# Expert stage of a decoder layer: first products two ahead of second ones, double buffers, early split of two experts' weights

## The reference, cut to what matters

```python
# x: (1024 tokens, 256), after a layer norm
logits = x @ gate_weight.T ; scores = sigmoid(logits)       # 16 routed experts
# two of four groups of experts by the sum of their two best, then the 4 best experts
weight = scores of the chosen ones / their sum * 2.5        # 0 for the others
y  = (silu(x @ sh_gate_w.T) * (x @ sh_up_w.T)) @ sh_down_w.T    # shared, width 256
for e in range(16):                                             # routed, width 128
    y += weight[:, e] * ((silu(x @ gate_w[e].T) * (x @ up_w[e].T)) @ down_w[e].T)
out = x_residual + y
```

## Time and profile before

| | us |
|---|---|
| median of three runs | 595.95 |
| the profiled execution, its own time | 597.41 |
| its span, first to last instruction | 595.5 |
| TensorE busy | 557.4 |
| ScalarE busy | 398.3 |
| VectorE busy | 437.1 |
| GpSimd busy | 298.9 |

### The profile page before, as it was taken

The page is one execution under the profiler, slowest core; times in us unless marked ns, Lnnn a source line. Parts: engine busy times, 40 slices in busy tenths (PEclk is TensorE's granted clock), DMA queues, the critical chain, the costliest instruction groups (busy, mean ns, idle before and its releaser), DMA issues.

```text
span 595.5 us, 10331 instructions
## 1 busy us (share of the span) xinstructions
PE 557.4 (94%) x3392; PEld 488.2 (82%) x3392; DVE 437.1 (73%) x1046; ACT 398.3 (67%) x783; POOL 298.9 (50%) x201
## 2 busy tenths in 40 slices
PE   3899999999999999999999999897777799999996
PEld 1687889989989989989989988786566688888885
DVE  8778989989989988998998998968593433333334
ACT  4978988878978979879779778665531433343331
POOL 2434756746746646656666563301041655556542
PEclk9998999999999999999999999999998899999999
DMA  6122032032032032032031020110002433333311
GB/s 206 29 107 81 0 117 81 1 116 81 2 117 81 2 116 81 2 116 75 8 116 56 27 97 23 59 29 1 0 1 70 149 105 107 104 123 113 108 62 70
DMA packets 16267, 42.23 MB, mean 71 GB/s; under 512 B 4544, under 2 KB 4800, under 8 KB 16224
## 3 DMA queue, kind: packets, MB, share of 16 engines
q1 hardware_dynamic: 16224, 41.69, 20.9%
HBM read 40.47 MB, written 1.21 MB: 70 GB/s over the span
## 4 chain that ended last, share of the span: by engine, by line
PE 83%; DVE 8%; ACT 4%; DMA 2%; issue 2%; SPq 1%; ACTq 0%; DVEq 0%
PE bank L1258 20%; PE bank L1260 19%; PE bank L1259 19%; PE bank L1254 15%; PE bank L1396 5%; PE bank L1384 4%; ACT tok L624 2%; DMA xbias<-in_xb 1%; DMA w_raw<-in_w 1%; DVE stats L976 1%; DVE xT_lo L911 1%; DVE gated_lo L1158 1%; ACT values L538 0%; DVE x L1248 0%; DVE raw L995 0%
## 5 line engine op out<-in xcount | busy, mean ns | idle before, releaser
L1258 PE MATMUL bank<-xT_lo,w_hi 128*128 128x512 f32 x336 | 140.0, 417 | 3.6 <-DVE conv L1149 1.3
L1260 PE MATMUL bank<-xT_hi,w_hi 128*128 128x512 f32 x336 | 132.3, 394 | 0.0
L1259 PE MATMUL bank<-xT_hi,w_lo 128*128 128x512 f32 x336 | 131.8, 392 | 0.0
L425 POOL TENSOR_TENSOR gated_lo<-gated,gated_hi 128x512 fp32r<-128x512 f32 x30 | 38.7, 1290 | 116.5 <-ACT gated_hi L644 112.8
L624 ACT ACTIVATE tok<-bank,nmr,rstd 128x128 f32<-128x128 f32 x256 | 91.0, 504 | 2.1 <-DVE nmr L891 2.1
L502 POOL TENSOR_TENSOR gate<-conv,tap 128x512 f32<-128x512 f32 x36 | 46.4, 1291 | 84.5 <-DVE conv L1149 71.4
L1258 PEld LDWEIGHTS bank<-xT_lo,w_hi 128*128 128x128 f32 x336 | 63.5, 189 | 18.8 <-DVE conv L995 3.2
L1260 PEld LDWEIGHTS bank<-xT_hi,w_hi 128*128 128x128 f32 x336 | 63.3, 188 | 14.2
L420 POOL TENSOR_TENSOR conv<-tap,conv 128x506 f32<-128x506 f32 x32 | 61.9, 1934 | 21.8 <-DVE conv L995 21.8
L420 POOL TENSOR_TENSOR raw<-tap,raw 128x506 f32<-128x506 f32 x32 | 61.9, 1934 | 20.3 <-DVE raw L995 16.3
L1259 PEld LDWEIGHTS bank<-xT_hi,w_lo 128*128 128x128 f32 x336 | 63.7, 190 | 9.6
(11 more groups left out here) (167 smaller groups left out, 1358.3 us busy)
## 6 DMA issues: line engine op xcount, KB each, us to landing
w_raw<-in_w SPq DMA_DIRECT2D x34, 384.0 KB, 4.4
obet<-obet_rows SPq DMA_DIRECT2D x16, 768.0 KB, 4.2
tap<-route_rows SPq DMA_DIRECT2D x16, 512.0 KB, 3.6
wv_raw<-in_wv SPq DMA_DIRECT2D x8, 256.0 KB, 4.8
wo_raw<-in_wo SPq DMA_DIRECT2D x8, 256.0 KB, 4.9
x<-in_x SPq DMA_DIRECT2D x2, 512.0 KB, 4.6
out_x<-x SPq DMA_DIRECT2D x4, 256.0 KB, 2.4
raw<-in_ctx SPq DMA_DIRECT2D x1, 512.0 KB, 5.4
```

Of the source, the lines that this page charges most:

```text
L425: nc.gpsimd.tensor_tensor(gated_lo[:, cc], gated[:, c * N:(c + 1) * N], gated_hi[:, cc].bitcast(F32), ALU.subtract).then_inc(gated_lo_read ...
L1258: nc.tensor.matmul(o, l_hi, r_lo, start=start, stop=False, skip_group_check=loose)
L1259: nc.tensor.matmul(o, l_lo, r_hi, start=False, stop=False, skip_group_check=loose)
L1260: return nc.tensor.matmul(o, l_hi, r_hi, start=False, stop=stop, skip_group_check=loose)
```

## The change

- The second products run one expert later: TensorE's order in the loop is `gate_up(n+2)`, `down(n)`.
- `silu_g`, `prod`, `act_hi`, `act_lo` and the product with the factors get two buffers (`two`, `weighted`).
- Experts 1 and 2 are not multiplied by a factor; their `act_hi` and `act_lo` are made from `prod`. The memset of ones goes.
- Experts 3 and 4 are split whole into memory that the attention leaves free (`early`), ahead of the last layer norm: ScalarE's `early_high` between `context_soft(1)` and `context_att(1)`, GpSimd's `early_low` after the first addition of the context. The weights of 5 and 6 are loaded right after, and split after `r_ready`.
- GpSimd does nothing from there to `r_ready`.
- ScalarE takes the sigmoid of half 0, the silu of expert 1's half 0, the sigmoid of half 1, the scores' copy, the silu of half 1. TensorE has the transposes of the scores before the last quarter of `gate_up(1)`, and the whole of `gate_up(3)` before `down(2)`.
- In the loop ScalarE's order is `gate_silu(n)`, `gate_up_high(n+1)`, `act_high(n)`, `down_high(n)`; GpSimd's `weigh(n,0)`, `gate_up_low(n+1)`, `weigh(n,1)`, `down_low(n)`; SyncE's factors of n, wait for `down_low(n)`, weights of n+2.

```diff
-        act_w = gate
-        act_hi, act_lo = gated_hi[:, 0:T], gated_lo[:, 0:T]
+        act_hi, act_lo = gated_hi[:, 0:2 * T], gated_lo[:, 0:2 * T]
+        def two(n, c):
+            return slice(n % 2 * T + c * N, n % 2 * T + (c + 1) * N)
+        def weighted(n, c):
+            if n <= E_SHARED:
+                return prod[:, two(n, c)]
+            o = n % 2 * 3 * T + c * N
+            return gate[:, o:o + N]
+        def early(n):
+            return (wv_hi[:, 64:64 + 3 * D], wv_lo[:, 64:64 + 3 * D]) if n == 3 else (
+                wo_hi[:, 0:3 * D], wo_lo[:, 0:3 * D])
...
             load_expert(4, 1)
+            for n in (5, 6):
+                sp.wait_ge(w_lo_ready, n - 2 + H)
+                load_expert(n, 1 - n % 2)
...
-            def load_route(e, s, before):
-                sp.wait_ge(e_weighted, before)
+            def load_route(e, s):
+                if not (isinstance(e, int) and e < 2):
+                    sp.wait_ge(e_weighted, e * NCH - NCH)
...
-            with sp.Fori(0, E_ROUTED // 2 - 1) as r:
+            with sp.Fori(0, E_ROUTED // 2 - 2) as r:
                 for s in range(2):
-                    expert_split(r * 2 + (3 + s))
-                    load_expert(r * 2 + (5 + s), s)
-                    load_route(r * 2 + (2 + s), s, r * (2 * NCH) + NCH * (3 + s))
+                    load_route(r * 2 + (2 + s), s)
+                    sp.wait_ge(down_lo_ready, r * 2 + (s + 1))
+                    load_expert(r * 2 + (7 + s), s)
+            for s in range(2):
+                load_route(E_ROUTED - 2 + s, s)
...
-            pool.wait_ge(p_added, TT // 2)
-            nc.gpsimd.memset(wbc, 1.0).then_inc(ones_ready, 1)
-            pool.wait_ge(ones_ready, 1)
-            weigh(1, 0, True)
-            gate_up_low(3, 0)
-            weigh(2, 1, False)
-            gate_up_low(4, 1)
-            down_low(3, 0)
-            def step(n, s, left=2):
-                pool.wait_ge(ld_route[s], (n - 1 - s) * 8)
-                weigh(n, s, False)
-                if left > 1:
-                    gate_up_low(n + 2, s)
-                if left > 0:
-                    down_low(n + 1, 1 - s)
+            pool.wait_ge(x_mixed, 1)
+            early_low(3)
+            early_low(4)
+            pool.wait_ge(r_ready, 1)
+            gate_up_low(5, 0)
+            gate_up_low(6, 1)
+            def step(n, m, s, up=True, down=True):
+                pool.wait_ge(ld_route[s], n * 8 - (1 + s) * 8)
+                weigh(n, m, s, 0)
+                if up:
+                    gate_up_low(n + 1, 1 - s)
+                weigh(n, m, s, 1)
+                if down:
+                    down_low(n, s)
+            step(3, 3, 0, False, False)
+            step(4, 4, 1, False, False)
+            step(5, 5, 0, False)
+            step(6, 6, 1)
...
             context_soft(1)
+            early_high(3)
+            early_high(4)
             context_att(1)
...
-            gate_silu(1, True, (0,))
+            router_scores(0)
+            gate_silu(1, 1, (0,))
+            router_scores(1)
             act.wait_ge(r_tok_full, 1)
...
+            def step(n, m, s, up=True):
+                gate_silu(n, m)
+                if up:
+                    gate_up_high(n + 1, 1 - s)
+                act_high(n, m)
+                down_high(n, s)
...
-                    u_times(r * 2 + (3 + s))
-                    act_low(r * 2 + (3 + s))
+                    u_times(r * 2 + (7 + s), 7 + s)
+                    act_low(r * 2 + (7 + s), 7 + s)
...
             pe.wait_ge(r_tr_ready, NCH)
-            gate_up(3, 0, chunks=(1,))
             gate_up(4, 1)
-            down(3, 0, False, False)
-            with pe.Fori(0, E_ROUTED // 2 - 1) as r:
+            gate_up(5, 0)
+            down(3, 3, 0)
+            gate_up(6, 1)
+            down(4, 4, 1)
+            with pe.Fori(0, E_ROUTED // 2 - 2) as r:
                 for s in range(2):
-                    gate_up(r * 2 + (5 + s), s)
-                    down(r * 2 + (4 + s), 1 - s, False, False)
-            down(E_ALL, 1, False, True)
+                    gate_up(r * 2 + (7 + s), s)
+                    down(r * 2 + (5 + s), 5 + s, s)
+            down(E_ALL - 1, E_ALL - 1, 0)
+            down(E_ALL, E_ALL, 1)
```

More of the change, by code:

```diff
@@ L488, in down_low @@
                 w = slice(s * 3 * D + 2 * D, (s + 1) * 3 * D)
-                pool.wait_ge(down_hi_ready, n - E_SHARED)
+                pool.wait_ge(down_hi_ready, n - 4)
                 nc.gpsimd.tensor_tensor(w_lo[:, w], w_raw[:, w], w_hi[:, w].bitcast(F32),
                                         ALU.subtract).then_inc(down_lo_ready, 1)
[L493 to L503, removed]
@@ L525, in _, with early_low, weigh @@
-            with pool.Fori(0, E_ROUTED // 2 - 1) as r:
+            def early_low(n):
+                hi, lo = early(n)
+                s = 1 - n % 2
+                pool.wait_ge(w_hi_ready, n + H)
+                nc.gpsimd.tensor_tensor(lo, w_raw[:, s * 3 * D:(s + 1) * 3 * D], hi.bitcast(F32),
+                                        ALU.subtract).then_inc(w_lo_ready, 1)
+            def weigh(n, m, s, c):
+                pool.wait_ge(u_prod, n * NCH + (c + 1 - NCH))
+                if not (isinstance(n, int) and n < 5):
+                    pool.wait_ge(e_hi, n * NCH + (c + 1 - 3 * NCH))
+                    pool.wait_ge(e_lo, n * NCH + (c + 1 - 3 * NCH))
+                nc.gpsimd.tensor_tensor(weighted(m, c), prod[:, two(m, c)],
+                                        wbc[:, s * T + c * N:s * T + (c + 1) * N],
+                                        ALU.mult).then_inc(e_weighted, 1)
@@ L802, in _, with router_scores @@
                 half_out(2, c, xT_hi)
-            for c in range(NCH):
+            def router_scores(c):
                 act.wait_ge(r_full, c + 1)
@@ L1211, in _ @@
             op(nc.vector.tensor_tensor(k4, k4, gm4, ALU.add))
-            act_low(1)
-            u_times(2, chunks=(0,))
+            u_times(2, 2, (0,))
+            act_low(1, 1)
             for t in range(TT):
@@ L1603, in down @@
-            def down(n, s, first, last):
-                if not (isinstance(n, int) and n <= E_SHARED):
-                    pe.wait_ge(down_lo_ready, n - E_SHARED)
-                o = s * 3 * D + 2 * D
-                for t in range(TT):
-                    if t % G == 0:
-                        pe.wait_ge(e_lo, (n - 1) * NCH + t // G + 1)
-                    tt = slice(t * P, (t + 1) * P)
-                    ins = mm3(y_acc[t // 2][:, (t % 2) * D:(t % 2 + 1) * D], act_hi[:, tt], act_lo[:, tt],
-                              w_hi[:, o:o + D], w_lo[:, o:o + D], first and t % 2 == 0, last, loose=True)
-                    if last and t % 2:
-                        ins.then_inc(y_full, 1)
-                if not last:
-                    ins.then_inc(e_down, 1)
+                hi, lo = w_hi[:, s * 3 * D:(s + 1) * 3 * D], w_lo[:, s * 3 * D:(s + 1) * 3 * D]
@@ new lines, in gate_up @@
+                if isinstance(n, int) and n in (3, 4):
+                    hi, lo = early(n)
+                for c, j in parts:
+                    if not (isinstance(n, int) and n == 1):
+                        pe.wait_ge(g_silu if j == 0 else u_prod, n * NCH + (c + 1 - 2 * NCH))
+                    for kt in range(KT):
+                        o = j * D + kt * P
+                        ins = mm3(e_ring[2 * c + j][:, :], hi[:, o:o + P], lo[:, o:o + P],
+                                  xs_(xT_hi, kt, c * N, (c + 1) * N), xs_(xT_lo, kt, c * N, (c + 1) * N),
+                                  kt == 0, kt == KT - 1)
+                    ins.then_inc(e_full, 1)
@@ new lines, in down @@
+            def down(n, m, s, chunks=range(NCH)):
+                hi, lo = w_hi[:, s * 3 * D:(s + 1) * 3 * D], w_lo[:, s * 3 * D:(s + 1) * 3 * D]
+                if m in (3, 4):
+                    hi, lo = early(m)
+                elif m > 4:
+                    pe.wait_ge(down_lo_ready, n - 4)
+                o = 2 * D
+                for c in chunks:
+                    pe.wait_ge(e_lo, n * NCH + (c + 1 - NCH))
+                    for t in range(G * c, G * (c + 1)):
+                        tt = slice(m % 2 * T + t * P, m % 2 * T + (t + 1) * P)
+                        ins = mm3(y_acc[t // 2][:, (t % 2) * D:(t % 2 + 1) * D], act_hi[:, tt], act_lo[:, tt],
+                                  hi[:, o:o + D], lo[:, o:o + D], m == 1 and t % 2 == 0, m == E_ALL, loose=True)
+                        if m == E_ALL and t % 2:
+                            ins.then_inc(y_full, 1)
+                    if m < E_ALL and c == NCH - 1:
+                        ins.then_inc(e_down, 1)
```

163 lines of the change are left out of this document (89 added, 74 removed).

## The result

The changed kernel takes 629.17 us (median of 4 runs, 626.52 to 631.81) against 595.96: 1.054 times the kernel before, 95% interval 1.048 to 1.060. It is slower, as forecast, but by 33 us and not by 18: above the range of 603 to 623. In a later round (e10_after) it took 627.05 (623.98 to 629.55), 1.052 times the kernel before (1.048 to 1.057). The profiled execution took 630.37 us, its span is 628.4.

What follows compares the result with a forecast made beforehand. TensorE, busy 94%, bounds the old kernel; a GpSimd transfer cycle bounds the changed loop. 467.4 + 11 x 10.95 = 587.9, plus 7.3 and 13.9 to 609.1, plus 0.8 and 3.7: span 613.6, forecast 614.0 us, range 603 to 623.

Steps and rivals of the forecast that it cites:

- What bounds the kernel before, and what could be won: TensorE, busy 94% of the span, at 8.27 us per expert; some 13 to 15 us winnable outside the loop.
- TensorE stays the bound: Rival for the expert loop: period stays 8.27 us, factors being there before GpSimd asks; 581.6 us, chance 0.03.
- Part 1: Early split of experts 3 and 4: ScalarE's 1.7 us hidden in idle time, GpSimd's subtractions priced at 0.
- Part 2: Routing stage: short VectorE operations with GpSimd idle, `r_ready` at 445.6 against 451.2; four table loads make TensorE wait 2 us.
- D5: End of the low part of down of expert 5, forecast at 467.4 (467.3 to 467.5).
- Part 3: Stretch from `gate_up(1)` to `down(4)`: no TensorE stall over 0.3 us besides the 2 us, ending about 472.6.
- Part 4: New queue order in the expert loop: factors held back until GpSimd's previous instruction, period 10.95 us, TensorE idle about 2.7.
- the ring: Loop cycle through SyncE's issues, the factors' transfer, GpSimd and ScalarE, independent of TensorE: 10.89 us, 10.95 with waking.
- issue of the weights to the start of `weigh`: Loop term for the second issue and the factors' landing: 4.6 us taken, between 4.0 and 6.0.
- The end: After D16: `gate_up(18)` starts 7.3 us later, last products 13.9 us plus 0.8 for the clock, then 3.7 to span's end.
- D16: End of the low part of down of expert 16, eleven periods after D5, forecast at 587.9.
- the second issue is held up: Rival: each factor transfer issued slowly or landing after 5.6 us; loop period 11.8 to 12.35, 623 to 629, chance 0.12.

Runs made afterwards that it cites:

- e10_after: The changed kernel itself, unaltered, measured again in a later round on the same chip as e9_unrolled: 627.05 us, 1.052 times the kernel before.
- e5_all: Changed kernel with factors issued one step earlier, down's split ahead of the second multiply and act_high, and both sigmoids together: 582.35 us, ratio 0.976.
- e8_busy: e5_all with seven unneeded 128x512 multiplies put on GpSimd in the routing: 586.16 us against 582.35.
- e9_unrolled: Changed kernel with SyncE's loop written out, order unchanged: 618.30 us, ratio 1.037.
- e2_swap: Changed kernel with the two issues behind the wait swapped, factors of n+1 before weights of n+2: 615.26 us, ratio 1.033.
- e1_ahead: Changed kernel with the factors of expert n+1 issued before the wait for down's low part of n: 588.87 us, ratio 0.988.
- e3_sigmoids: Changed kernel with ScalarE's two sigmoids one after the other and the first silu behind them: 624.89 us, ratio 1.047.
- e6_half: Changed kernel loading only the factors of the first 512 tokens, used by both halves: 612.83 us, ratio 1.025.

## Why the prediction was right or wrong

- *What bounds the kernel before, and what could be won*: right. With everything in order (e5_all) the time is 582.35; the rival "TensorE stays the bound" had 581.6.
- *Part 1*, the early split at no cost: right. ScalarE's idle time ahead of `L722` is 0.35 us after, where it was 1.81, and the layer norm isn't later.
- *Part 2*, the routing on VectorE: right. I had `r_ready` at 445.6; it came at 445.48, and `L1228`, the old `L1179`, takes 0.29 us and not 1.22. e8_busy shows that it is GpSimd's idleness that does it.
- *Part 2*, four table loads: the 2 us of waiting came as 1.92, and no drain follows a load, as in the earlier trace rows. Against the 2.8 us more that I had estimated from the Trainium skill (ScalarE: Activation LUTs, "What ACT_TABLE_LOAD costs") the trace of after decides:

```profile
424.71 1.28 ACT L844 ACT_TABLE_LOAD   x1
426.01 0.59 ACT L844 ACTIVATE gate<-bank 16x512 f32<-16x512 f32 x1
426.61 1.28 ACT L813 ACT_TABLE_LOAD   x1
427.91 0.60 ACT L813 ACTIVATE tok<-bank 128x512 f32<-128x512 f32 x1
428.52 1.28 ACT L844 ACT_TABLE_LOAD   x1
429.82 0.59 ACT L844 ACTIVATE gate<-bank 16x512 f32<-16x512 f32 x1
```

- Here a term was missing: the granted clock falls behind this wait (last section). TensorE's order therefore ran 1.3 us late, and the routing weights were ready at 451.15, not 449.9. The trip of the factors over DRAM took 6.94 us, not 5.95; in the other traces with whole factors it varies from 5.6 to 8.0. Together D5 is 469.55 instead of 467.4: 2.15 us.
- *Part 3*, the stretch to `down(4)`: right. TensorE has no wait there besides the 1.92 us, and ends `down(4)` near 474.1, where I had 472.6; `gate_up(2)` already ended 1.3 us late.
- *Part 4*, the ring: right in what it goes through, and in its independence of TensorE. It was mis-sized. The sum had 10.95; the mean of eleven periods is 11.81:

| term | predicted | measured |
|---|---|---|
| end of down's low part to issue of the weights | 0.18 | 0.17 |
| distance of the two issues | 0.40 | 0.75 (0.62 and 0.90 in turn) |
| issue of the factors to `weigh` | 4.26 | 4.71 |
| GpSimd's and ScalarE's work to the end of down's low part | 6.11 | 6.17 |

  The step that failed is "issue of the weights to the start of `weigh`", for which I took 4.6 us between 4.0 and 6.0, 4.66 with the wait to wake, and which is 5.46. Of the 0.80 us too little, 0.35 is the distance of the two issues: "0.33 us of issuing and some register work" undervalued that work, and e9_unrolled takes it out (0.37). The other 0.45 lies between the issue of the factors and their use. That my 4.26 was not far off for two transfers in flight together is shown by e9_unrolled (4.37) and by e2_swap's order (4.25); it is 4.71 in the profiled execution of after and 4.53 in e10_after, and why it is longer there stays open. The last row agrees by luck in part: the second multiply took 1.73 and not 1.54, the low part of down, which no longer meets `act_low`, 0.94 and not 1.02, and the two operations before them 0.02 us less each. The period is 0.86 us longer, and eleven of them make 9.4 us.
- *The end*: the last pair of factors was issued back to back, with the weights of 18 just ahead, and the factors of 17 needed 6.34 us (5.03 in e10_after), so that `gate_up(18)` started 9.68 us behind D16, not 7.3 (2.4 us more). The last products took 15.7 us and not 14.7, as the clock fell behind a wait of 4.67 us:

```profile
609.10 0.79 PE L1315 MATMUL bank<-xT_lo,w_hi 128*128 128x512 f32 x1 [4.67 <-POOL w_lo L499]
```

- Sum: 2.15 + 9.4 + 2.4 + 1.0 = 15.0, and 613.6 + 15.0 is the measured span of 628.4 within 0.3 us. Every one of the four went the same way, so nothing cancelled.
- *The range*: the rival "the second issue is held up" had the right size for the wrong reason. No issue took 1.4 us, the longest is 0.43. (Its lower end of 11.8 follows from neither of its figures: an issue of 1.376 us gives a period of 12.0, a landing of 5.6 gives 12.35.) I gave 0.12 to all that lay above 623, though the upper bound of my own unknown, 6.0 us instead of 4.6, gave 614.0 + 11 x 1.4 = 629 by itself; the bounds of a term that counts eleven times should have gone into the range whole.

## What to carry to other kernels

When a queue is reordered, walk once round each buffer and write down who must finish before the next issue of it: a transfer that is queued behind a wait for an engine's last instruction, and needed by that engine's next one, puts its whole latency into every period. A fixed cost in such a ring is multiplied by the number of rounds, so it deserves its upper bound in the range, and the issuing engine's arithmetic and the other transfers in flight belong to it. The cure is an order in which the transfer is issued one step earlier, and work that needs no result of the step goes ahead of what does.

## What the runs showed of the hardware

- TensorE's clock falls behind waits that I had thought too short. In `after` TensorE waits 1.92 us for the second sigmoid, with full clock and matmuls before it, and then has its eight small transposes. TensorE's timeline and two windows of after, with the columns of the earlier trace rows:

```profile
430.45 0.66 PE L1694 MATMUL bank<-ident,gate 16*128 16x16 f32 x8 [1.92 <-ACT gate L844]
...
432.59 0.63 PE L1316 MATMUL bank<-xT_hi,w_lo 128*128 128x512 f32 x1
433.02 0.63 PE L1317 MATMUL bank<-xT_hi,w_hi 128*128 128x512 f32 x1
```

```profile
432.00:434.00 2.00, 2.00 (x6) 1.52 (x6) 1.83 (x12) 1.85 (x3) 0.00 (x0) 0.50 0.00 0
436.00:438.00 2.00, 2.00 (x10) 1.65 (x9) 1.27 (x4) 0.81 (x2) 0.00 (x0) 1.00 0.00 0
```

  From 431.5 to 434.9 the clock is at its lower level, matmuls start 0.43 us apart and not 0.23, and 1.7 us are lost. In the traces with this wait the clock fell in six of eight; the other two, e1_ahead and e2_swap, had come back from the lower clock at 426.0 and 427.6 us, some 5 us before the wait began, where the six had full clock for 10 us and more. In the three traces without the wait (e3_sigmoids, e5_all, e8_busy) the clock never fell there. In the loop of `after` the lower clock came behind each of the six waits of 3.45 us and more, and behind none of the six of 2.87 us and less:

```profile
501.20 0.49 PE L1315 MATMUL bank<-xT_lo,w_hi 128*128 128x512 f32 x1 [2.87 <-POOL w_lo L499]
...
513.65 0.79 PE L1315 MATMUL bank<-xT_lo,w_hi 128*128 128x512 f32 x1 [3.89 <-POOL w_lo L499]
514.24 0.63 PE L1316 MATMUL bank<-xT_hi,w_lo 128*128 128x512 f32 x1
```

  With the 1.92 us of the routing beside the 2.87 us of the loop, a wait's length alone doesn't tell.
- In the ring of `after` two rounds of a loop differ by their place: the factors issued across the end of a round come 0.28 us later after the weights, and their landing takes longer too: from issue to use 4.88 us against 4.57, and 4.89 against 4.22 in e10_after (most periods are 11.4 to 11.5 and 12.0 to 12.4 in turn). The first part is the loop's register work. The landing hardly alternates in e9_unrolled, 4.45 against 4.29, where rows and buffers are the same but the two issues always lie equally far apart. So rows and buffer explain little of it; how the distance of the issues could act on the landing, no run tells.
- Whether a kernel whose period holds a transfer scatters more is not shown: the four runs of `after` span 5.3 us and those of e10_after 5.6, but those of e9_unrolled 2.8 and of e6_half 2.6, and those of e5_all, without a transfer in its period, 4.6.
